# Attention on one core: the causal mask of the diagonal maxima, by mask products on TensorE or inside VectorE's fused sum-and-maximum

## The chip, the cores and the metric

The kernel runs on 1 core of one Trainium2 chip. The metric is the device time of one execution in microseconds (us), and the number to predict is the median of several executions.

## What is computed

One transformer layer in fp32: a layer norm, causal attention with 16 heads of 16 dimensions, a residual, a second layer norm, a ternary two-layer MLP with a low-rank addition, and a second residual. Input is x of (4, 2048, 256). The change concerns the attention alone:

```python
qkv = x @ W_attn + b_attn
q, k, v = jnp.split(qkv, 3, axis=2)          # 16 heads of 16
scores = jnp.einsum('bhqd,bhkd->bhqk', qh, kh) * 0.25
causal = jnp.tril(jnp.ones((S, S), dtype=bool))
scores = jnp.where(causal, scores, -jnp.inf)
probs = jax.nn.softmax(scores, axis=-1)
out = jnp.einsum('bhqk,bhkd->bhqd', probs, vh)
```

## The kernel before

Four parts run one after another: the preparation of the weights (`build_prep`), the layer norm with the q, k, v products (`build_qkv`), the attention (`build_attention`), and the output projection with the MLP (`build_mlp`). Every engine's program is written out by hand, in order, with semaphores between them.

The attention works in 16 units of one batch and four heads (`UNITS`; a pair index p = 0, 1 and a row half r = 0, 1 name the head). Queries and keys lie in chunks of 512 (`CH`), four to a unit, each of four tiles of 128. The softmax needs each query's largest score first, so every unit goes through two passes over the scores.

The maxima. A unit has 68 items (`MAXES`, `NM`). One item is formed on TensorE (`form_max`, line 1019) into one of two slots of `ps_m` (`SLOTS` = 2, two banks of 512 columns each, one per r), and VectorE takes the maximum over the keys out of it (`reduce_max`, line 967) into one column of `maxes`. 48 items lie below the diagonal: one query tile against 512 keys, for the two heads of a pair, reduced by a single VectorE instruction over 2 x 512 elements (line 976). 20 items, five to a chunk, touch the diagonal: two of width 512 (query tile 3), two that hold a piece of 384 and a piece of 128 columns (query tiles 2 and 0), and one that holds two pieces of 256 (query tile 1, both pairs). Their last 128 columns are the triangle. For these TensorE adds the mask itself: behind the scores of a piece come four bf16 products of an identity half with a mask half (line 1037), which accumulate -1e30 above the diagonal. VectorE then reduces them like the others: line 976 where the pieces are equally wide, line 979 otherwise, twice an item. `slot_filled` tells VectorE that an item is formed, and `slot_freed` tells TensorE that it is reduced. `find_max` (line 983) makes the negative maximum of a chunk; GpSimd and TensorE turn it into rows that are stored beside the queries.

The second pass. A unit has 36 steps (`STEPS`, `NS`). A full step forms the scores of one key tile for 512 queries and four heads in four banks (`scores`, line 1056, a ring `ps_s` of three banks), ScalarE takes the exponential of each bank (line 953), and TensorE multiplies the probabilities of three steps before by the values (`values`, line 1072, into `ps_acc`). Four of the 36 steps are half steps with two banks. GpSimd zeroes the triangle of the probabilities (line 891).

What sets the order. `order(s, last)` interleaves the two passes: a full step is bank 0, bank 1, one item, bank 2, values, bank 3, one more item; a half step is two banks, values, one item. The items run 40 ahead of the steps (`LEAD`), so 40 items of the first unit are formed and reduced before its first step: the opening.

The mask. `build_prep` makes `ident` and `mask` on GpSimd (lines 229 to 234) and bf16 copies of both. In `build_qkv` ScalarE's queue issues eight DMAs (line 658) that bring halves of them to the partitions where the mask products want them; they stand between the copies of the first chunk and the square root of the second (`norm.take_root(act, 1)`, line 661).

Of the kernel before, what the change touches and what calls it, by code (L numbers as in the profile page):

```python
# [25 lines left out]
BF16 = mybir.dt.bfloat16  # L26
ALU = mybir.AluOpType
# [52 lines left out]
def banks_of(s):  # L80

    return GH // STEPS[s][1]

# [95 lines left out]
def build_prep(nc, io, keep):  # L181

    with ExitStack() as ctx:
# [14 lines left out]
        w1 = t.sb("w1_sum", [P, KD, HID])  # L198
        w_qkv, w_o = t.sb("w_qkv_in", [P, KD, 3 * DIM]), t.sb("w_o_in", [P, KD, DIM])
        scale_rows = t.sb("scale_rows", [P, KD, P])  # L200
        mask = t.sb("mask", [P, P])
        ps = t.ps("ps_prep", [P, 8, 512])
        loaded, fc_in, proj_in = t.sem("prep_loaded"), t.sem("fc_in"), t.sem("proj_in")
        masked = t.sem("prep_masked")
# [21 lines left out]
        @block.gpsimd  # L226
        def _(pool):

            pool.memset(keep["ident"][:], 0.0)
            pool.memset(mask[:], 0.0).then_inc(masked, 1)  # L230
            pool.wait_ge(masked, 1)
            pool.affine_select(out=keep["ident"][:], in_=keep["ident"][:], compare_op=ALU.not_equal, fill=1.0,
                               base=0, pattern=[[-1, P]], channel_multiplier=1)
            pool.affine_select(out=mask[:], in_=mask[:], compare_op=ALU.is_ge, fill=NEG,
                               base=0, pattern=[[-1, P]], channel_multiplier=1).then_inc(masked, 1)
            pool.wait_ge(masked, 2)
            pool.tensor_copy(keep["ident_h"][:], keep["ident"][:])
            pool.tensor_copy(keep["mask_h"][:], mask[:]).then_inc(masked, 1)

        @block.vector  # L240
        def _(dve):
# [80 lines left out]
        @block.tensor  # L322
        def _(pe):
            pe.wait_ge(loaded, 16 * 9)
            pe.wait_ge(masked, 3)
            for n in range(KH):
                pe.transpose(ps[0:RANK, n // 4, (n % 4) * P:(n % 4 + 1) * P], u_in[:, n, :], keep["ident"][:])
            pe.transpose(ps[0:RANK, 2, 0:RANK], fast[:], keep["ident"][0:RANK, 0:RANK]).then_inc(done_pe, 1)

            pe.wait_ge(done_act, 1)  # L330
            pe.matmul(ps[0:RANK, 3, 0:DIM], fast_t[:], v_in[:], start=True, stop=True).then_inc(done_pe, 1)

            pe.wait_ge(done_act, 2)
            for k in range(KD):
                for half in range(2):
                    last = pe.matmul(ps[:, 4 + 2 * k + half, :], g_mat[:, k * P:(k + 1) * P],
                                     u_t[:, half * 512:half * 512 + 512], start=True, stop=True)
            last.then_inc(done_pe, 1)

            pe.wait_ge(done_act, 4)  # L340
            pe.wait_ge(chain, N_TERNARY)
            for k in range(KD):
                for half in range(2):
                    for n in range(4):
                        last = pe.transpose(ps[:, 4 + 2 * k + half, n * P:(n + 1) * P],
                                            fc_a[:, 4 * half + n, k * P:(k + 1) * P], keep["ident"][:])
                    last.then_inc(done_pe, 1)
            for n in range(KH):
                for k in range(KD):
                    col = n * DIM + k * P  # L350
                    last = pe.transpose(ps[:, col // 512, col % 512:col % 512 + P],
                                        proj_a[:, k, n * P:(n + 1) * P], keep["ident"][:])
            last.then_inc(done_pe, 1)

            pe.wait_ge(chain, N_SUM)
            for k in range(KD):
                last = pe.transpose(ps[:, 4, k * P:(k + 1) * P], scale_rows[:, k], keep["ident"][:])
            last.then_inc(done_pe, 1)
# [135 lines left out]
class Shared:  # L494
# [3 lines left out]
    def __init__(self, nc, ctx):  # L498
        t = Tensors(nc, ctx)

        self.qs, self.ks = t.sb("qs0", [P, NCH, PAIRS, CH], F32R), t.sb("ks0", [P, NCH, PAIRS, CH], F32R)
        self.vs = t.sb("vs0", [P, KT, GH, VW])
        self.v_in = t.sb("v_dense", [P, KT, GH * HD])
        self.probs = t.sb("probs", [P, RING, GH, CH])
        self.ones = t.sb("ones", [ROW, ROW])
        self.ident_half = t.sb("ident_half", [P, 2, P], BF16)
        self.mask_half = t.sb("mask_half", [P, 2, P], BF16)
        self.ones_set, self.fixed_in = t.sem("ones_set"), t.sem("fixed_in")
        self.stack_in = [[t.sem(f"stack_in{i}_{c}") for c in range(NCH)] for i in range(2)]
        self.v_loaded, self.v_ready = t.sem("v_loaded"), t.sem("v_spread")  # L510
        self.parts_stored = [t.sem(f"parts_stored{i}") for i in range(2)]
        self.v_stored = [t.sem(f"v_stored{i}") for i in range(2)]
# [31 lines left out]
            act.dma_start(ks[row:row + 1].bitcast(F32).rearrange("o c p (x e) -> o (c p x) e", e=ROW), sh.ones[:]).then_inc(sh.fixed_in, 16)  # L544

FIXED = 2 * MROWS + 2 * 2 * 2

PRELOAD, PRELOADED = 8, 4

# [1 line left out]
def build_qkv(nc, io, keep, scr, sh):  # L552

    with ExitStack() as ctx:
# [95 lines left out]
        @block.scalar  # L650
        def _(act):
            norm.take_root(act, 0)
            copy_high(act, xn_t[0], ps_t, xt_ready, xt_copied, 0)

            for r in range(2):
                for half in range(2):
                    for dst, src in ((sh.ident_half, keep["ident_h"]), (sh.mask_half, keep["mask_h"])):
                        act.dma_start(dst[ROW * r:ROW * (r + 1), half], src[ROW * half:ROW * (half + 1), :]).then_inc(sh.fixed_in, 16)
            act.wait_ge(sh.ones_set, 1)
            load_ones(act, sh, sh.ks)  # L660
            norm.take_root(act, 1)

            def body(n, used, u, left):
                if left >= 2:

                    act.wait_ge(xn_ready, n + 1)
                    load(act, n + 2, u)
                if left >= 1:

                    copy_high(act, xn_t[1 - u], ps_t, xt_ready, xt_copied, KD * (n + 1))
                if left >= 2:
                    norm.take_root(act, n + 2)
                for m in range(4):
                    act.wait_ge(qk_ready, 4 * n + m + 1)
                    if m == 0 and not zero(used):

                        act.wait_ge(parts_stored[u], 16 * 4 * used)
                    act.activation(parts[u][:, m, 0], ps_qk[:, m], ACT.Identity, bias=keep["b_qk"][:, m:m + 1]
                                   ).then_inc(qk_copied, 1)  # L680

            over_chunks(act, body)
# [44 lines left out]
def build_attention(nc, io, keep, scr, sh):  # L727

    with ExitStack() as ctx:
# [1 line left out]
        qs = [sh.qs, t.sb("qs1", [P, NCH, PAIRS, CH], F32R)]  # L731
        ks = [sh.ks, t.sb("ks1", [P, NCH, PAIRS, CH], F32R)]
        vs = [sh.vs, t.sb("vs1", [P, KT, GH, VW])]
        probs, ident_half, mask_half, stack_in = sh.probs, sh.ident_half, sh.mask_half, sh.stack_in
        maxes = [t.sb(f"maxes{i}", [P, 2, PAIRS, TT, NCH]) for i in range(2)]
        neg_max = [t.sb(f"neg_max{i}", [P, 2, PAIRS * TT]) for i in range(2)]
        max_parts = [t.sb(f"max_parts{i}", [P, 2, MROWS, PAIRS * TT], F32R) for i in range(2)]
# [229 lines left out]
        def _(dve):  # L967
            def reduce_max(n, k):
                c, pieces = MAXES[k]
                slot = k % SLOTS  # L970
                dve.wait_ge(slot_filled, NM * n + k + 1)
                if pieces[0][4] == pieces[-1][4]:
                    (_, tt, i, _, width) = pieces[0]
                    pairs = slice(pieces[0][0], pieces[-1][0] + 1)
                    banks = ps_m[:, 2 * slot:2 * slot + 2].rearrange("q r (p x) -> q r p x", x=width)
                    last = dve.tensor_reduce(maxes[c % 2][:, :, pairs, tt, i], banks, AX.X, ALU.max)  # L976
                else:
                    for p, tt, i, col, width in pieces:
                        last = dve.tensor_reduce(maxes[c % 2][:, :, p, tt, i], ps_m[:, 2 * slot:2 * slot + 2, col:col + width],  # L979
                                                 AX.X, ALU.max)  # L980
                last.then_inc(slot_freed, 1)

            def find_max(n, c):
# [34 lines left out]
        def _(pe):  # L1018
            def form_max(n, par, k):
# [8 lines left out]
                for p, tt, i, col, width in pieces:  # L1028
                    for r in range(2):
                        rows = slice(ROW * r, ROW * r + TERMS)  # L1030
                        last = pe.matmul(ps_m[:, 2 * slot + r, col:col + width], qs[par][rows, c, p, tt * P:(tt + 1) * P],  # L1031
                                         ks[par][rows, i, p, 0:width], start=True, stop=(i < c), skip_group_check=True)
                    if i == c:
                        for half in range(2):
                            for r in range(2):
                                rows = slice(ROW * r, ROW * (r + 1))
                                last = pe.matmul(ps_m[:, 2 * slot + r, col + width - P:col + width], ident_half[rows, half],  # L1037
                                                 mask_half[rows, half], start=False, stop=(half == 1), skip_group_check=True)
                last.then_inc(slot_filled, 1)

            def turn_rows(n, c, k):
# [345 lines left out]
def build_layer(nc, io):  # L1387
    with ExitStack() as ctx:
# [8 lines left out]
            "b_v": t.sb("b_v", [P, DIM]),  # L1397
            "b_o": t.sb("b_o", [P, DIM]),
            "ident": t.sb("ident", [P, P]),
            "ident_h": t.sb("ident_h", [P, P], BF16),  # L1400
            "mask_h": t.sb("mask_h", [P, P], BF16),
        }
        scr = {
            "q": nc.dram_tensor("q_scr", [BATCH, PARTS, DIM, SEQ], F32).ap(),
# [38 lines left out]
```

## Time and profile before

| | us |
|---|---|
| median of 3 executions | 2171.63 |
| lowest and highest | 2161.71, 2176.84 |
| the profiled execution | 2175.73 |
| its span, first to last instruction | 2174.0 |
| TensorE busy | 2060.0 (95%) |
| VectorE busy | 1818.3 (84%) |
| ScalarE busy | 1460.1 (67%) |
| GpSimd busy | 473.6 (22%) |

### The profile page before, as it was taken

The numbers are of one execution on the slowest core, as the hardware profiler recorded it, in microseconds if no ns is written. First come the engines' busy times: TensorE is split into PE (matmuls) and PEld (weight loads), VectorE is DVE, ScalarE is ACT, GpSimd is POOL, SyncE is SP. The second block draws the span as 40 slices with busy tenths as digits, with TensorE's granted clock in tenths as the row PEclk, the third lists the DMA queues.
The fourth block names the chain that finished last, engine by engine and source line by source line (L and its number), as shares of the span: only waits on it lengthen the run. The fifth ranks groups of instructions, "written<-read, shape, count | busy, mean of one in ns | idle before, by whom it ended". The sixth has DMA issues, their size and how long they took to land. (4 is left out here: it accounts for less than half of the span.)

```text
span 2174.0 us, 40441 instructions
## 1 busy us (share of the span) xinstructions
PE 2060.0 (95%) x15605; PEld 1202.4 (55%) x15605; DVE 1818.3 (84%) x2365; ACT 1460.1 (67%) x2800; POOL 473.6 (22%) x637
## 2 busy tenths in 40 slices
PE   3999799999999999999999999999999949999998
PEld 2887354544545445454444544444454228888887
DVE  6898888888888888888888888888888018998996
ACT  1333078887878788787787887878878625555554
POOL 0000011110111101111011111111111027776674
PEclk8999589999999999999999999999999759999999
DMA  2799121311213212122221212212120023232320
GB/s 86 260 315 342 63 58 37 78 46 51 56 37 79 52 51 56 37 73 51 59 55 37 67 49 66 50 42 63 46 69 17 11 82 85 81 101 84 88 78 30
DMA packets 162977, 167.92 MB, mean 77 GB/s; under 512 B 74704, under 2 KB 102880, under 8 KB 162784
## 3 DMA queue, kind: packets, MB, share of 16 engines
q1 hardware_dynamic: 154112, 157.72, 24.9%
q10 hardware_dynamic: 8672, 7.60, 1.2%
q8 instruction: 123, 2.02, 0.4%
q14 instruction: 70, 0.57, 0.1%
HBM read 95.77 MB, written 67.63 MB: 75 GB/s over the span
## 5 line engine op out<-in xcount | busy, mean ns | idle before, releaser
L953 ACT ACTIVATE probs<-ps_s 128x512 f32<-128x512 f32 x2176 | 1144.5, 601 | 291.7 <-PE ps_s L1068 282.3
L976 DVE TENSOR_REDUCE maxes<-ps_m 128x2 f32<-128x1024 f32 (+1 forms) x960 | 1136.5, 1218 | 139.6 <-PE ps_m L1031 104.0
L1068 PE MATMUL ps_s<-qs,ks 50*128 50x512 f32 (+3 forms) x2560 | 810.3, 416 | 8.6 <-ACT probs L953 8.5
L1031 PE MATMUL ps_m<-ks,qs 48*128 48x512 f32 (+3 forms) x2560 | 715.9, 426 | 15.6 <-DVE maxes L976 9.6
L1068 PEld LDWEIGHTS ps_s<-qs,ks 50*128 50x128 f32 x2560 | 404.0, 189 | 510.4 <-ACT probs L953 461.5
L1087 PE MATMUL ps_acc<-probs,vs 128*32 128x512 f32 (+3 forms) x5120 | 598.5, 549 | 0.7
L1031 PEld LDWEIGHTS ps_m<-ks,qs 48*128 48x128 f32 x2560 | 362.4, 190 | 105.8 <-issue 49.5
L891 POOL TENSOR_SCALAR_AFFINE_SELECT probs<-probs 128x512 f32<-128x512 f32 x256 | 157.6, 637 | 753.0 <-ACT probs L953 753.0
L1037 PE MATMUL ps_m<-mask_half,ident_half 64*128 64x128 bf16 x2048 | 207.4, 227 | 0.0
L1087 PEld LDWEIGHTS ps_acc<-probs,vs 128*32 128x32 f32 x5120 | 109.3, 109 | 160.1 <-issue 98.1
L1240 POOL TENSOR_TENSOR hid<-square,hid 128x512 fp32r<-128x512 f32 x128 | 174.6, 1372 | 105.8 <-DVE square L1251 93.4
L979 DVE TENSOR_REDUCE maxes<-ps_m 128x2 f32<-128x768 f32 (+1 forms) x256 | 161.6, 685 | 28.7 <-PE ps_m L1037 28.2
L1360 PE MATMUL ps_y<-w,hid 128*128 128x256 f32 x1024 | 131.8, 284 | 6.7 <-POOL hid L1240 6.7
L879 POOL CAST max_parts<-neg_max 128x16 fp32r<-128x16 f32 x64 | 12.7, 198 | 573.9 <-DVE neg_max L985 573.9
L1313 ACT ACTIVATE relu<-ps_h 128x512 f32<-128x512 f32 x128 | 76.4, 597 | 88.8 <-PE ps_h L162 80.0
L1360 PEld LDWEIGHTS ps_y<-w,hid 128*128 128x128 f32 x1024 | 125.4, 188 | 11.5 <-POOL hid L1240 10.1
L1251 DVE TENSOR_TENSOR square<-relu 128x512 f32<-128x512 f32 x96 | 96.5, 1012 | 26.4 <-ACT relu L1313 25.4
L160 PE MATMUL ps_h<-mxn_t,w 128*128 128x512 f32 x256 | 102.3, 400 | 1.5 <-DVE mxn_t L491 1.4
L1037 PEld LDWEIGHTS ps_m<-mask_half,ident_half 64*128 64x128 bf16 x2048 | 94.2, 98 | 15.7 <-issue 5.2
L162 PE MATMUL ps_h<-mxn_t,w 128*128 128x512 f32 x256 | 101.8, 398 | 0.0
L161 PE MATMUL ps_h<-mxn_t,w 128*128 128x512 f32 x256 | 101.6, 397 | 0.0
L1318 ACT ACTIVATE hid<-relu 128x512 fp32r<-128x512 f32 x128 | 81.0, 633 | 4.1
(129 smaller groups left out, 1635.7 us busy)
## 6 DMA issues: line engine op xcount, KB each, us to landing
qs<-q_scr SPq DMA_DIRECT2D x384, 64.0 KB, 2.7
ks<-k_scr SPq DMA_DIRECT2D x384, 64.0 KB, 2.7
q_scr<-probs SPq DMA_DIRECT2D x32, 512.0 KB, 4.4
k_scr<-probs SPq DMA_DIRECT2D x32, 512.0 KB, 5.6
o_scr<-acc_sb SPq DMA_DIRECT2D x64, 256.0 KB, 2.9
v_scr<-probs SPq DMA_DIRECT2D x16, 512.0 KB, 6.1
v_dense<-v_scr SPq DMA_DIRECT2D x16, 512.0 KB, 4.6
o_in<-o_scr SPq DMA_DIRECT2D x32, 256.0 KB
```

Of the source, the lines that this page charges most:

```text
L160: pe.matmul(out, sh, mh, start=start, stop=False)
L162: return pe.matmul(out, sl, mh, start=False, stop=stop)
L891: pool.affine_select(out=tile, in_=tile, compare_op=ALU.is_ge, fill=0.0, base=0, pattern=[[0, GH], [1, P]], channel_multiplier=-1).then_in ...
L953: act.activation(probs[:, s % RING, x], ps_s[:, k % BANKS], ACT.Exp).then_inc(ring_taken, 1)
L976: last = dve.tensor_reduce(maxes[c % 2][:, :, pairs, tt, i], banks, AX.X, ALU.max)
L979: last = dve.tensor_reduce(maxes[c % 2][:, :, p, tt, i], ps_m[:, 2 * slot:2 * slot + 2, col:col + width], AX.X, ALU.max)
L1031: last = pe.matmul(ps_m[:, 2 * slot + r, col:col + width], qs[par][rows, c, p, tt * P:(tt + 1) * P], ks[par][rows, i, p, 0:width], start=T ...
L1037: last = pe.matmul(ps_m[:, 2 * slot + r, col + width - P:col + width], ident_half[rows, half], mask_half[rows, half], start=False, stop=(h ...
L1068: last = pe.matmul(ps_s[:, k % BANKS, at:at + width], ks[u][rows, j // TT, p, j % TT * P:(j % TT + 1) * P], qs[u][rows, c, p, q0:q0 + widt ...
L1087: last = pe.matmul(ps_acc[h * VW:(h + 1) * VW, q0:q0 + width], vs[u][:, j, h], probs[:, s % RING, h % banks_of(s), at:at + width], start=( ...
L1240: pool.tensor_tensor(hid[:, 1, m], square[:, m], hid[:, 0, m].bitcast(F32), ALU.subtract).then_inc(low_done, 1)
L1360: last = pe.matmul(ps_y[:, i, (tt % 2) * DIM:(tt % 2 + 1) * DIM], hid[:, a, m, tt * P:(tt + 1) * P], keep["w2"][:, m], start=(m == 0 and a ...
```

## The change

VectorE adds the mask to the diagonal pieces while it takes their maximum: `tensor_tensor_reduce` computes (scores + mask) x 1.0, writes it to a scratch tile `sums_masked`, and puts the maximum over it into one column of `maxes`. It takes one head at a time, so each piece needs two of them (r = 0, 1). The mask is a tile of 128 x 512, zero but for the triangle in its last 128 columns, and a piece of width w reads its last w columns. Since scratch is used again by the next diagonal item, VectorE waits before each such item until its own last instruction of the item before is done (`slot_freed`). TensorE's mask products go, and with them the halves of identity and mask, their bf16 copies and their eight DMAs.

```diff
@@ build_prep, GpSimd
-            pool.memset(mask[:], 0.0).then_inc(masked, 1)
+            pool.memset(keep["mask"][:], 0.0).then_inc(masked, 1)
...
-            pool.affine_select(out=mask[:], in_=mask[:], compare_op=ALU.is_ge, fill=NEG,
+            pool.affine_select(out=keep["mask"][:, CH - P:], in_=keep["mask"][:, CH - P:], compare_op=ALU.is_ge, fill=NEG,
                                base=0, pattern=[[-1, P]], channel_multiplier=1).then_inc(masked, 1)
-            pool.wait_ge(masked, 2)
-            pool.tensor_copy(keep["ident_h"][:], keep["ident"][:])
-            pool.tensor_copy(keep["mask_h"][:], mask[:]).then_inc(masked, 1)
@@ build_qkv, ScalarE
-            for r in range(2):
-                for half in range(2):
-                    for dst, src in ((sh.ident_half, keep["ident_h"]), (sh.mask_half, keep["mask_h"])):
-                        act.dma_start(dst[ROW * r:ROW * (r + 1), half], src[ROW * half:ROW * (half + 1), :]).then_inc(sh.fixed_in, 16)
             act.wait_ge(sh.ones_set, 1)
             load_ones(act, sh, sh.ks)
@@ build_attention
+        sums_masked = t.sb("sums_masked", [P, 4, CH])
@@ build_attention, VectorE, reduce_max
                 dve.wait_ge(slot_filled, NM * n + k + 1)
-                if pieces[0][4] == pieces[-1][4]:
-                    (_, tt, i, _, width) = pieces[0]
-                    pairs = slice(pieces[0][0], pieces[-1][0] + 1)
-                    banks = ps_m[:, 2 * slot:2 * slot + 2].rearrange("q r (p x) -> q r p x", x=width)
-                    last = dve.tensor_reduce(maxes[c % 2][:, :, pairs, tt, i], banks, AX.X, ALU.max)
+                if pieces[0][2] < c:
+                    (p, tt, i, _, _), = pieces
+                    last = dve.tensor_reduce(maxes[c % 2][:, :, p, tt, i], ps_m[:, 2 * slot:2 * slot + 2], AX.X, ALU.max)
                 else:
+
+                    if NM * n + k > 0:
+                        dve.wait_ge(slot_freed, NM * n + k)
                     for p, tt, i, col, width in pieces:
-                        last = dve.tensor_reduce(maxes[c % 2][:, :, p, tt, i], ps_m[:, 2 * slot:2 * slot + 2, col:col + width],
-                                                 AX.X, ALU.max)
+                        for r in range(2):
+                            last = dve.tensor_tensor_reduce(sums_masked[:, 2 * pieces.index((p, tt, i, col, width)) + r, 0:width], ps_m[:, 2 * slot + r, col:col + width],
+                                                            keep["mask"][:, CH - width:], 1.0, NEG, ALU.add, ALU.max,
+                                                            maxes[c % 2][:, r, p, tt, i:i + 1])
                 last.then_inc(slot_freed, 1)
@@ build_attention, TensorE, form_max
-                                         ks[par][rows, i, p, 0:width], start=True, stop=(i < c), skip_group_check=True)
-                    if i == c:
-                        for half in range(2):
-                            for r in range(2):
-                                rows = slice(ROW * r, ROW * (r + 1))
-                                last = pe.matmul(ps_m[:, 2 * slot + r, col + width - P:col + width], ident_half[rows, half],
-                                                 mask_half[rows, half], start=False, stop=(half == 1), skip_group_check=True)
+                                         ks[par][rows, i, p, 0:width], start=True, stop=True, skip_group_check=True)
```

How instructions stand on VectorE at the first diagonal of the opening (items of width 512 and 512, then the two of 384 and 128 columns). Before:

```order
350 L976 TENSOR_REDUCE maxes<-ps_m 128x2 [waits slot_filled] x2
351 L979 TENSOR_REDUCE maxes<-ps_m 128x2 [waits slot_filled]
352 L979 TENSOR_REDUCE maxes<-ps_m 128x2
353 L979 TENSOR_REDUCE maxes<-ps_m 128x2 [waits slot_filled]
354 L979 TENSOR_REDUCE maxes<-ps_m 128x2
```

Here a diagonal item is one or two reductions, each over both heads. In the changed kernel, from the second item of width 512 to the end of the first of 384 and 128 columns, the same engine has (ISA is the name these rows give to the parts of a `tensor_tensor_reduce`):

```order
354 L974 ISA sums_masked,maxes<-ps_m,mask 128x512 [waits slot_freed,slot_filled]
355 L974 ISA maxes 128x1
356 L974 ISA sums_masked,maxes<-ps_m,mask 128x512
357 L974 ISA maxes 128x1
358 L974 ISA sums_masked,maxes<-ps_m,mask 128x384 [waits slot_freed,slot_filled]
359 L974 ISA maxes 128x1
360 L974 ISA sums_masked,maxes<-ps_m,mask 128x384
361 L974 ISA maxes 128x1
362 L974 ISA sums_masked,maxes<-ps_m,mask 128x128
363 L974 ISA maxes 128x1
364 L974 ISA sums_masked,maxes<-ps_m,mask 128x128
365 L974 ISA maxes 128x1
```

An item of width 512 has become four instructions, one of 384 and 128 columns eight: each sum-and-maximum is followed by one that writes a single column of `maxes`.

TensorE before, the first chunk of the opening (items of width 512, 512, 384 and 128):

```order
816 L1031 MATMUL ps_m<-ks,qs 128x512 [waits stack_in0_0,fixed_in]
817 L1031 MATMUL ps_m<-ks,qs 128x512
818 L1037 MATMUL ps_m<-mask_half,ident_half 128x128 x4
819 L1031 MATMUL ps_m<-ks,qs 128x512 x2
820 L1037 MATMUL ps_m<-mask_half,ident_half 128x128 x4
821 L1031 MATMUL ps_m<-ks,qs 128x384 [waits slot_freed]
822 L1031 MATMUL ps_m<-ks,qs 128x384
823 L1037 MATMUL ps_m<-mask_half,ident_half 128x128 x4
824 L1031 MATMUL ps_m<-ks,qs 128x128 x2
825 L1037 MATMUL ps_m<-mask_half,ident_half 128x128 x4
```

And the same place of the changed kernel:

```order
816 L1027 MATMUL ps_m<-ks,qs 128x512 [waits stack_in0_0,fixed_in]
817 L1027 MATMUL ps_m<-ks,qs 128x512 x3
818 L1027 MATMUL ps_m<-ks,qs 128x384 [waits slot_freed]
819 L1027 MATMUL ps_m<-ks,qs 128x384
820 L1027 MATMUL ps_m<-ks,qs 128x128 x2
```

The mask products are gone and nothing else moved; the waits for a free slot stand where they stood.

## Rows read from the trace of the kernel before

**Rows 1.** Busy time by stretch: opening and body of the attention's maxima.

```profile
core 0: us, PE busy (x) PEld busy (x) DVE busy (x) ACT busy (x) POOL busy (x), PEclk, DMA share, GB/s
223.00:275.00 52.00, 40.93 (x211) 20.90 (x212) 48.51 (x51) 4.32 (x9) 3.09 (x8) 0.50 0.07 24
275.00:1688.00 1413.00, 1408.88 (x11849) 686.34 (x11851) 1252.14 (x1290) 1134.82 (x2216) 191.58 (x383) 1.00 0.20 53
```

**Rows 2.** VectorE groups by form: busy us, mean ns, idle before them.

```profile
L976 DVE TENSOR_REDUCE maxes<-ps_m 128x2 f32<-128x1024 f32 x896 | 1059.9, 1218 | 125.3 <-PE ps_m L1031 104.0 <-PE ps_m L1037 16.2
L979 DVE TENSOR_REDUCE maxes<-ps_m 128x2 f32<-128x768 f32 x128 | 122.1, 954 | 28.7 <-PE ps_m L1037 28.2
L976 DVE TENSOR_REDUCE maxes<-ps_m 128x4 f32<-128x1024 f32 x64 | 78.2, 1221 | 14.3 <-PE ps_m L1037 14.3
L979 DVE TENSOR_REDUCE maxes<-ps_m 128x2 f32<-128x256 f32 x128 | 53.2, 416 | 0.0
...
L644 DVE TENSOR_TENSOR probs<-ps_v,b_v 128x256 f32<-128x256 f32 x64 | 22.7, 414 | 1.3 <-PE ps_v L162 1.3
...
L491 DVE TENSOR_TENSOR xn_t<-ps_t,xn_t 128x512 fp32r<-128x512 f32 x32 | 20.7, 681 | 4.1 <-ACT xn_t L484 4.0
```

**Rows 3.** Mask products on TensorE, by form.

```profile
L1037 PE MATMUL ps_m<-mask_half,ident_half 64*128 64x128 bf16 x2048 | 207.4, 227 | 0.0
```

**Rows 4.** TensorE timeline, value products alone: the start of each step.

```profile
1034.63 1.07 PE L1087 MATMUL ps_acc<-probs,vs 128*32 128x384 f32 x16
1037.24 0.64 PE L1087 MATMUL ps_acc<-probs,vs 128*32 128x256 f32 x8
1039.76 1.06 PE L1087 MATMUL ps_acc<-probs,vs 128*32 128x512 f32 x8
1042.62 1.06 PE L1087 MATMUL ps_acc<-probs,vs 128*32 128x512 f32 x8
...
1053.85 1.07 PE L1087 MATMUL ps_acc<-probs,vs 128*32 128x512 f32 x8
```

**Rows 5.** VectorE timeline: steps below the diagonal, then the diagonal of a chunk.

```profile
1024.51 2.36 DVE L976 TENSOR_REDUCE maxes<-ps_m 128x2 f32<-128x1024 f32 x2 [0.31 <-PE ps_m L1031]
1027.12 2.36 DVE L976 TENSOR_REDUCE maxes<-ps_m 128x2 f32<-128x1024 f32 x2 [0.24 <-PE ps_m L1031]
...
1041.84 2.48 DVE L979 TENSOR_REDUCE maxes<-ps_m 128x2 f32<-128x768 f32 x4 [0.72 <-PE ps_m L1037]
1044.71 2.36 DVE L976 TENSOR_REDUCE maxes<-ps_m 128x4 f32<-128x1024 f32 x2 [0.38 <-PE ps_m L1037]
...
1055.63 1.23 DVE L976 TENSOR_REDUCE maxes<-ps_m 128x2 f32<-128x1024 f32 x1 [0.41 <-PE ps_m L1031]
```

**Rows 6.** VectorE timeline of the opening, second chunk.

```profile
231.65 0.17 DVE L985 TENSOR_REDUCE neg_max<-maxes 128x16 f32<-128x16 f32 x1
231.74 10.36 DVE L976 TENSOR_REDUCE maxes<-ps_m 128x2 f32<-128x1024 f32 x9
242.44 2.48 DVE L979 TENSOR_REDUCE maxes<-ps_m 128x2 f32<-128x768 f32 x4 [0.35 <-PE ps_m L1037]
```

**Rows 7.** VectorE timeline in the q, k, v part: two-operand and small instructions.

```profile
63.75 0.16 DVE L406 TENSOR_TENSOR tmp_attn<-rstd_attn 128x4 f32<-128x4 f32 x1
63.94 0.16 DVE L408 TENSOR_TENSOR tmp_attn<-tmp_attn,var_attn 128x4 f32<-128x4 f32 x1
...
68.48 1.41 DVE L644 TENSOR_TENSOR probs<-ps_v,b_v 128x256 f32<-128x256 f32 x4
70.03 1.29 DVE L491 TENSOR_TENSOR xn_t<-ps_t,xn_t 128x512 fp32r<-128x512 f32 x2
```

**Rows 8.** Timeline of ScalarE, its queue and VectorE around the eight DMAs.

```profile
47.52 0.54 ACTq L658 DMA_DIRECT2D ident_half<-ident_h  x1
...
50.70 0.17 DVE L401 TENSOR_SCALAR var_attn<-mv_attn 128x4 f32<-128x4 f32 x1
...
51.97 0.62 ACTq L658 DMA_DIRECT2D mask_half<-mask_h  x1
52.63 2.55 ACTq L544 DMA_DIRECT2D ks<-ones  x4
55.22 0.20 ACT L421 ACTIVATE root_attn<-var_attn 128x4 f32<-128x4 f32 x1 [7.12 <-issue]
```

More of the change, by code:

```diff
@@ L200, in build_prep @@
         scale_rows = t.sb("scale_rows", [P, KD, P])
-        mask = t.sb("mask", [P, P])
         ps = t.ps("ps_prep", [P, 8, 512])
@@ L324, in _ @@
             pe.wait_ge(loaded, 16 * 9)
-            pe.wait_ge(masked, 3)
+            pe.wait_ge(masked, 2)
             for n in range(KH):
@@ L505, in __init__ @@
         self.ones = t.sb("ones", [ROW, ROW])
-        self.ident_half = t.sb("ident_half", [P, 2, P], BF16)
-        self.mask_half = t.sb("mask_half", [P, 2, P], BF16)
         self.ones_set, self.fixed_in = t.sem("ones_set"), t.sem("fixed_in")
@@ L544, in load_ones @@
             act.dma_start(ks[row:row + 1].bitcast(F32).rearrange("o c p (x e) -> o (c p x) e", e=ROW), sh.ones[:]).then_inc(sh.fixed_in, 16)
-FIXED = 2 * MROWS + 2 * 2 * 2
+FIXED = 2 * MROWS
 PRELOAD, PRELOADED = 8, 4
@@ L733, in build_attention @@
         vs = [sh.vs, t.sb("vs1", [P, KT, GH, VW])]
-        probs, ident_half, mask_half, stack_in = sh.probs, sh.ident_half, sh.mask_half, sh.stack_in
+        probs, stack_in = sh.probs, sh.stack_in
+        sums_masked = t.sb("sums_masked", [P, 4, CH])
         maxes = [t.sb(f"maxes{i}", [P, 2, PAIRS, TT, NCH]) for i in range(2)]
@@ L1399, in build_layer @@
             "ident": t.sb("ident", [P, P]),
-            "ident_h": t.sb("ident_h", [P, P], BF16),
-            "mask_h": t.sb("mask_h", [P, P], BF16),
+            "mask": t.sb("mask", [P, CH]),
         }
```

## The prediction

> **What bounds the kernel now.** I read the busy times by stretch first. The opening of the attention (52 us) is VectorE's: it is busy 48.5 us of it, and TensorE's clock is 0.50, its lower level of 1.2 GHz, while it waits for slots. The body (1413 us) looks like TensorE's, busy 1409 us, at clock 1.00 [rows 1]. But VectorE is busy 1252 us of the same 1413, so it has only 161 us to spare, 11%. In such a case the mean share decides nothing, and I look at the steps.
>
> A step's length is the distance between starts of value products: 2.61 us from 1034.63 to 1037.24 for a step below the diagonal, 2.86 us from 1039.76 to 1042.62 for one that holds two items of 384 and 128 columns, and 14.09 us for the five steps from 1039.76 to 1053.85 [rows 4]. On VectorE a step below the diagonal is two reductions and a gap of 0.24 us that ends when TensorE has formed the next item; at the diagonal the gap is 0.38 to 0.72 us and ends with a mask product of line 1037 [rows 5]. So below the diagonal VectorE waits for TensorE by a quarter of a microsecond per step, and at the diagonal by a little more: the mask products do sit on the path, but VectorE is almost as late. Over the trace VectorE's idle time that line 1037 ends is 16.2 + 28.2 + 14.3 = 58.7 us [rows 2]. TensorE's 207.4 us of mask products [rows 3] are no measure of what they cost, since two row halves run side by side and most of it lies beside other products.
>
> **What the masks cost on the path.** Five steps with diagonal items took 14.09 us against 5 x 2.61 = 13.05: 1.04 us, or 0.21 a step [rows 4]. They hold seven diagonal items, so one chunk (five items) costs about 0.7 us, and 64 chunks 45 us. That is the most that taking them away can bring, if nothing becomes later.
>
> **What VectorE pays instead.** All distances are from start to start where no wait stands between, which is what a queue pays. Before, one reduction of 1024 elements: nine take 10.36 us [rows 6], the last counting in full with 1.22 us [rows 2], so (10.36 - 1.22) / 8 = 1.14 us. An item of 384 and 128 columns is two reductions: with 0.08 us of overlap each, (0.954 - 0.08) + (0.416 - 0.08) = 1.21 us [rows 2]. A chunk's five diagonal items: 3 x 1.14 + 2 x 1.21 = 5.84 us.
>
> After, each piece is done once per head. The nearest rows for one such instruction are additions or subtractions of a bank in PSUM and a tile in SBUF: 512 columns, two in 1.29 us of which the last is 0.68, so 0.61 us; 256 columns, four in 1.41 us, the last 0.41, so 0.33 us [rows 2, 7]. The slope is 1.09 ns a column; 384 columns then cost 0.47 us and 128 cost 0.19 us. A chunk has four of each width: 4 x (0.61 + 0.47 + 0.33 + 0.19) = 6.40 us. That is already more than before, since 16 instructions replace 7.
>
> Second, the order shows a further instruction behind each of the 16, which puts one column into `maxes`. No row shows one like it. From below: a reduction of 16 values, after which the next instruction starts 0.09 us later (231.65 to 231.74) [rows 6]; from above: the read waits until the sum has run out (0.07 us, the overlap that is lost between 0.68 and 0.61) and the next waits for the read's full 0.16 us, which is a small instruction's duration [rows 7], together 0.23 us. The lowest bound is that it costs nothing. I take 0.125 us, halfway between 0.09 and 0.16 (the read waits for the sum but nothing waits for the read), because no row decides between these two: 16 x 0.125 = 2.0 us.
>
> Third, the new wait on `slot_freed`: VectorE waits for the end of its own last instruction. With such waits, small instructions start 0.19 us apart (63.75 to 63.94) [rows 7], against 0.09 without one [rows 6]: 0.10 to 0.12 us, five times a chunk, 0.55 us. Behind the waiting instruction in VectorE's queue stand the other items, `neg_max` (for which GpSimd and then TensorE's row transposition wait, many steps ahead of need) and the reciprocals.
>
> The Trainium skill speaks against charging that wait: by its page "VectorE: DVE Perf Modes", section "The DRAIN you can't avoid", an instruction drains the pipe before the next in any case, and a semaphore between two adds nothing. The trace does not agree for small instructions (0.19 us with a wait, 0.09 without) [rows 6, 7]; by the page's rule the sum below would be 64 x 0.55 = 35 us less. The same page, in "Rules for kernel authors", advises fewer instructions over fused ones, which is what the count of 32 for 7 here goes against.
>
> Sum: 6.40 + 2.0 + 0.55 = 8.95 us a chunk against 5.84, so 3.11 us more, and 64 x 3.11 = 199 us more work on VectorE.
>
> **What hides part of it.** There are only two slots, so an item that is late holds up TensorE two items later; TensorE stands in front of the slot and with it the next bank, ScalarE's exponentials and the value products, and steps below the diagonal can't catch up, because they are bound by the loop of TensorE and ScalarE (their 2.61 us has 0.24 us of gap on VectorE, 9%). So only idle time right at the diagonal items is filled. That is the 58.7 us ended by line 1037, less some 5 us before the very first item, so 54 us, and one gap behind the last diagonal item of each chunk, 0.41 us at 1055.63 [rows 5], 64 x 0.41 = 26 us. Together 80 us. 199 - 80 = 119 us longer. The mask products' own gain is inside this: it is the idle time that VectorE now fills.
>
> The three diagonals of the opening are in the sum as others are; there VectorE is last by the whole.
>
> **The rest.** ScalarE's queue issues the eight DMAs from 47.52 until 52.6, then those of the ones; the square root for the second chunk, whose variance was ready at 50.87, starts at 55.22 after no wait but "issue" [rows 8]. Without the eight it starts at about 51.0: 4 us earlier, and VectorE's second normalisation with it. I take 4 us off; it may be 0 if the later stores of this part set its end. GpSimd's mask is four times as wide, but two conversions are gone, at the start of the kernel where nothing waits for it: nothing. The MLP is as before.
>
> Against the profiled execution: 2175.7 + 119 - 4 = 2290.7 us. The median of the runs is 4 us lower than that execution, by which the sum is 2286.6; the difference is well inside the 15 us between the lowest and the highest run, and I put 2290.
>
> **Rivals.**
>
> *Serial reads.* Each sum-and-maximum and each read run to their ends: 0.23 us instead of 0.125, 16 x 0.105 x 64 = 108 us more: 2400. For it: a value that is read out must be complete. Against: VectorE's other neighbours overlap by 0.07 to 0.09 us without a wait.
>
> *Half the rate.* If the fused instruction takes two cycles a column where it has a second tensor and a running maximum, 4 x 1280 columns x 1.09 ns = 5.6 us a chunk more, 357 us: about 2650. No row shows such an instruction; the additions of [rows 7] run at one column per 1.09 ns with an SBUF tensor beside PSUM. The Trainium skill has such a rule on its page "Vector Engine (DVE) Microarchitecture Reference", section "Points that are easy to get wrong", for two sources in SBUF wider than bf16 with an accumulator; here one source is PSUM, and no run so far shows which way it falls.
>
> *Faster, VectorE hidden.* If the one-column instruction and the wait cost nothing, VectorE's excess is 6.40 - 5.84 = 0.56 us a chunk, less than the 80 / 64 = 1.25 us of idle time that stands at the diagonals. Then TensorE is last there, and what counts is the mask products' 0.7 us: 2175.7 - 45 - 4 = 2127. The point from which it decides is (1.25 - 0.56) / 16 = 0.04 us per read, wait included. Against it: every small instruction in the trace costs at least 0.09.
>
> *Little change.* The read costs the 0.09 us and the wait nothing, and more idle time is filled than I count, say 1.9 of the 2.5 us that the body's 161 us are per chunk: 6.40 + 1.44 - 5.84 - 1.9 = 0.1 us a chunk: about 2180.
>
> *The clock falls.* While VectorE needs 3.9 us for a step of two 384-and-128 items, TensorE works under 2 us of it. In the opening, waiting for slots, its clock is at 1.2 GHz [rows 1]. If it fell at each diagonal, a step's value products of 1.06 us would take twice as long, three steps a chunk, 64 x 3 x 1.06 = 204 us at most: up to 2495.
>
> **Chances.** Forecast, with its own range of 2235 to 2350: 0.56. Serial reads: 0.18. Half the rate: 0.06. Clock: 0.05. Cheaper than forecast but over 1% slower (reads at 0.09 us or less and more hidden, 2195 to 2235): 0.07. Little change: 0.04. Faster: 0.04. The range 2210 to 2420 leaves out the last two, half the rate and most of the clock's case. About 1% is what a measurement of this kernel can tell from no change: faster 0.04, same 0.04, slower 0.92.
>
> **What would show it.** Right: line 974 with 1024 long instructions of 0.68, 0.54, 0.41 and 0.28 us and 1024 short ones; VectorE busy above 95% in the body; no idle time ended by a mask product; TensorE's weight loads waiting for `maxes` of line 974; steps at diagonals of 3.0 to 3.9 us, below them 2.6 as before; the square root near 51 us. Wrong: long instructions of twice these lengths, a clock below 1.00 in the body, or steps of 2.6 us at the diagonal.

## The result, and the profile after

| | us |
|---|---|
| median after (4 executions, 2197.2 to 2214.9) | 2206.53 |
| median before, beside it | 2174.24 |
| ratio | 1.0142, 95% interval 1.0107 to 1.0177 |
| the same pair measured again later (6 executions) | 2207.72, ratio 1.0174, 1.0130 to 1.0218 |
| profiled execution, its span | 2214.9, 2213.1 |

The change makes the kernel 1.4% slower, 32 us, where 2290 us was forecast, 116 us slower, with a range that began at 2210. The sign was right and the size was not. Beside the kernel before as it ran then, the second comparison gives 40 us. Ratios are formed from fast executions alone (one of e3_before_no_masks, 2159.11 us, and one of the kernel before beside g1 to g3, 2194.71 us, were slow), so they are not exactly the quotients of the medians.

The second stretch of [rows 1], in the profile after:

```profile
275.00:1688.00 1413.00, 1357.37 (x9563) 594.71 (x9565) 1272.58 (x2727) 1102.14 (x2149) 183.95 (x371) 0.99 0.20 53
```

TensorE is busy 51 us less of this stretch and VectorE only 20 us more: 1273 of 1413, 90%, not the 95% that I named. (The changed kernel runs longer, so the same window holds a little less of its work.) VectorE's groups at the diagonal, by form:

```profile
L974 DVE CUSTOM_DVE_ANT_0 sums_masked<-ps_m,mask 128x512 f32<-128x512 f32 x256 | 166.7, 689 | 23.5 <-PE ps_m L1027 7.9 <-DVE maxes L974 1.0 <-issue 0.7
...
L974 DVE DVE_READ_ACCUMULATOR2_ANT maxes<- 128x1 f32 x1024 | 84.9, 83 | 0.0
...
L974 DVE CUSTOM_DVE_ANT_0 sums_masked<-ps_m,mask 128x128 f32<-128x128 f32 x256 | 63.5, 285 | 0.0
```

The long instructions last what the additions of [rows 2] do, one column per 1.05 ns (0.689 and 0.285 us for 512 and 128 columns), so the rival of half the rate is out. The reads have 83 ns each, 85 us in all, but the sum of busy times hides where they lie. The timeline of the opening shows it (start, duration):

```profile
226.93 0.56 DVE L974 CUSTOM_DVE_ANT_0 sums_masked<-ps_m,mask 128x384 f32<-128x384 f32 x1
227.41 0.08 DVE L974 DVE_READ_ACCUMULATOR2_ANT maxes<- 128x1 f32 x1
227.41 0.55 DVE L974 CUSTOM_DVE_ANT_0 sums_masked<-ps_m,mask 128x384 f32<-128x384 f32 x1
...
228.31 0.08 DVE L974 DVE_READ_ACCUMULATOR2_ANT maxes<- 128x1 f32 x1
228.54 0.56 DVE L974 CUSTOM_DVE_ANT_0 sums_masked<-ps_m,mask 128x384 f32<-128x384 f32 x1
```

A read starts at the same time as the next long instruction (both 227.41), so its 83 ns are no price. Whether it moves that start at all can't be told here; e5_no_read measures it. Where there is a wait, from 228.31 to 228.54, 0.23 us pass that would not without it. Such an item takes 1.61 us (226.93 to 228.54), of which the wait is a seventh.

The starts of steps at a diagonal, to be read beside [rows 4], are 2.98 and 3.16 us apart here:

```profile
1067.19 1.06 PE L1077 MATMUL ps_acc<-probs,vs 128*32 128x512 f32 x8
1070.17 1.06 PE L1077 MATMUL ps_acc<-probs,vs 128*32 128x512 f32 x8
1073.33 1.06 PE L1077 MATMUL ps_acc<-probs,vs 128*32 128x512 f32 x8
```

and TensorE's loads now stand behind a slot that line 974 has not freed:

```profile
PEld ps_m L1027 <- DVE maxes L974: 127.3, 180, 1.7
```

The cleanest ruler is the distance between the last `neg_max` of one unit and of the next, since a unit is the same work each time. After (two units):

```profile
981.54 0.21 DVE L981 TENSOR_REDUCE neg_max<-maxes 128x16 f32<-128x64 f32 x1
1075.60 0.21 DVE L981 TENSOR_REDUCE neg_max<-maxes 128x16 f32<-128x64 f32 x1
```

Before:

```profile
955.20 0.21 DVE L985 TENSOR_REDUCE neg_max<-maxes 128x16 f32<-128x64 f32 x1
1046.98 0.21 DVE L985 TENSOR_REDUCE neg_max<-maxes 128x16 f32<-128x64 f32 x1
```

94.06 against 91.78 us: 2.28 us a unit, 34 us over the 15 distances between the first such instruction and the last. The first comes 8 us later (320.51 against 312.46). The eight DMAs that are gone give nothing back in this pair of profiles: the first product of the maxima starts at 223.19 us, and at 222.84 before.

### The profile page after: what moved, and what is told of

Same layout as the page of the kernel before. It is cut to its first block and busy times, and to the rows that moved or that the text cites. A ratio compares the mean times of both kernels' runs of the same rounds, so it can differ in the third digit from the quotient of the medians.

```text
span 2213.1 us, 38254 instructions
## 1 busy us (share of the span) xinstructions
PE 2038.7 (92%) x13557; PEld 1123.0 (51%) x13557; DVE 1880.7 (85%) x3965; ACT 1461.4 (66%) x2800; POOL 471.9 (21%) x635
## 5 line engine op out<-in xcount | busy, mean ns | idle before, releaser
L967 DVE TENSOR_REDUCE maxes<-ps_m 128x2 f32<-128x1024 f32 x768 | 911.0, 1218 | 99.7 <-PE ps_m L1027 92.4
L1058 PE MATMUL ps_s<-qs,ks 50*128 50x512 f32 (+3 forms) x2560 | 778.6, 406 | 9.5 <-ACT probs L946 9.5
L1027 PE MATMUL ps_m<-ks,qs 48*128 48x512 f32 (+3 forms) x2560 | 667.2, 426 | 75.6 <-DVE maxes L974 61.1
L974 DVE CUSTOM_DVE_ANT_0 sums_masked<-ps_m,mask 128x512 f32<-128x512 f32 (+3 forms) x1024 | 446.8, 488 | 51.1 <-PE ps_m L1027 7.9
L1027 PEld LDWEIGHTS ps_m<-ks,qs 48*128 48x128 f32 x2560 | 311.2, 191 | 213.2 <-DVE maxes L974 127.3
L974 DVE DVE_READ_ACCUMULATOR2_ANT maxes<- 128x1 f32 x1024 | 84.9, 83 | 0.0
L989 DVE RECIPROCAL recip<-sums 128x16 f32<-128x16 f32 x64 | 15.5, 243 | 65.4 <-DMA sums<-acc_sb 65.4
```

The lines of the kernel that those rows point to most:

```text
L974: last = dve.tensor_tensor_reduce(sums_masked[:, 2 * pieces.index((p, tt, i, col, width)) + r, 0:width], ps_m[:, 2 * slot + r, col:col + w ...
L1058: last = pe.matmul(ps_s[:, k % BANKS, at:at + width], ks[u][rows, j // TT, p, j % TT * P:(j % TT + 1) * P], qs[u][rows, c, p, q0:q0 + widt ...
```

## The experiments

Each ran beside the kernel before on one chip: e1 to e4 on one, e5 to e8 on another, g1 to g3 on a third. "Unit" is the distance just shown, read in each profile. It is the surest comparison across chips, since the medians also carry TensorE's mean granted clock, which differs from execution to execution. In the ten executions of the changed kernel it runs from 0.970 (2196.87 us) to 0.960 (2210.75 to 2214.90 us), about 1.7 us for each 0.001; 37 executions of the kernel before lie on a line of 1.6 us for each 0.001. Differences "at equal clock" below are my estimates by these two lines. They assume that a change acts beside the clock and not through it.

| run | what it is | median us | ratio to before | unit us |
|---|---|---|---|---|
| changed kernel | | 2206.53 | 1.0142 | 94.06 |
| e1_two_scratch | changed, the wait made idle | 2135.35 | 0.9807 | 90.38 |
| e2_before_wait | before, wait added | 2184.45 | 1.0036 | 92.25 |
| e3_before_no_masks | before, no mask products | 2136.59 | 0.9791 | 89.71 |
| e4_both_masks | changed, mask products kept | 2215.06 | 1.0172 | 94.17 |
| e5_no_read | changed, no read of the maximum | 2204.48 | 1.0124 | 93.12 |
| e6_dmas_back | changed, eight DMAs kept | 2218.57 | 1.0188 | 93.87 |
| e7_no_masks_wait | e3 with the wait | 2160.26 | 0.9918 | 90.42 |
| e8_last_unit_busy | e1 with products for nobody in the last unit | 2141.14 | 0.9828 | 90.43 |

**The wait alone, taken off the changed kernel** (e1_two_scratch). Two halves of scratch, used in turn; the wait is for the item before the last one, which is done by then.

```diff
-        sums_masked = t.sb("sums_masked", [P, 4, CH])
+        sums_masked = t.sb("sums_masked", [P, 8, CH])
...
-                    if NM * n + k > 0:
-                        dve.wait_ge(slot_freed, NM * n + k)
+                    half = 4 * (sum(j % NM in DIAGONAL_ITEMS for j in range(NM * n + k)) % 2)
+                    if NM * n + k > 1:
+                        dve.wait_ge(slot_freed, NM * n + k - 1)
```

> The changed kernel with twice the scratch, used in turn by the diagonal items, so that VectorE waits for the end of the item before the last one and not of the last one. Theory V (VectorE's time at the diagonals sets the loss: per chunk four of each width, 6.6 us, plus five waits of 0.22 us, 1.1 us): the waits are free, VectorE's time falls by 320 x 0.22 = 70 us, its excess over the kernel before is 0.8 us a chunk and is filled by idle time, and the time falls below both kernels, to 2136 to 2165 us. Theory N (the loss comes from the sixteen fused instructions themselves, and the wait lies in time that is lost anyway): 2195 to 2210 us, as the changed kernel.

Measured 2135.35 us, 71 us under the changed kernel and 1.9% under the kernel before. The unit is 3.68 us shorter, 59 us over 16, and 59 us is also the difference at equal clock; the rest of the 71 is a higher clock (0.966 to 0.972, against 0.960 to 0.968). The wait was the whole loss and more: without it the change is a gain. In its timeline the four 384 and 128 pieces follow at their plain distances; the next item starts 0.21 us after the last and not 0.21 + 0.23:

```profile
224.69 0.28 DVE L976 CUSTOM_DVE_ANT_0 sums_masked<-ps_m,mask 128x128 f32<-128x128 f32 x1
224.90 0.08 DVE L976 DVE_READ_ACCUMULATOR2_ANT maxes<- 128x1 f32 x1
224.90 0.55 DVE L976 CUSTOM_DVE_ANT_0 sums_masked<-ps_m,mask 128x384 f32<-128x384 f32 x1
```

**The same wait, added to the kernel before** (e2_before_wait).

```diff
                 dve.wait_ge(slot_filled, NM * n + k + 1)
+                if pieces[0][2] == c and NM * n + k > 0:
+                    dve.wait_ge(slot_freed, NM * n + k)
```

> The kernel before with nothing but the added wait of VectorE for its own last item, ahead of each diagonal item. Theory V: 320 waits of 0.22 us are 70 us of VectorE, of which the idle time at the diagonals (about 80 us) hides most: 2174 to 2190 us. Theory N: a wait for the engine's own last instruction costs nothing: 2174 us. If the waits lie on the path in full: 2244 us.

2184.45 us, 5 us over before (ratio 1.0036, 1.0011 to 1.0061), and 7 us by the unit and at equal clock. The same waits that cost 59 us there cost 7 here: most of each falls into the idle time that ends with a mask product.

**TensorE's mask products alone** (e3_before_no_masks). The four products behind each diagonal piece are left out and the reductions kept, so the maxima of diagonal pieces run over later keys as well.

> The kernel before without the mask products on TensorE (line 1037); the reductions stay, so the maxima of the diagonal pieces run over later keys too, and the mask is left out of them. What the mask products cost on the path by themselves. By the step lengths of the trace of before (0.21 us a step, 0.7 us a chunk): 45 us, 2120 to 2140 us. If VectorE's reductions are last there and the products lie beside them: 2165 to 2174 us.

2136.59 us, 43 us less. That looks like the estimate of 45 from step lengths, but the unit is only 2.07 us shorter, 33 us over 16, and the difference at equal clock is 35 us: the estimate was about 10 us too high. VectorE, unmasked, is hidden here: this is about the floor that taking the masks away can reach. e1's median is at it, but only because its executions had a higher clock: its unit is 0.67 us longer, and at equal clock it is 28 us under before where e3 is 35.

**Both at once** (e4_both_masks): the fused VectorE code with the mask products kept.

> The changed VectorE code with the mask products of TensorE kept (and their eight DMAs): the mask is added twice. Theory V: VectorE is last at the diagonals of the changed kernel, so TensorE has room for the products and only a part of their 45 us shows: 2215 to 2235 us. If the two costs simply add: 2250 us.

2215.06 us, 9 us over the changed kernel, and its unit is only 0.11 us longer (2 us over 16; this kernel also has the eight DMAs). Where VectorE is last, TensorE's products are nearly free. Removing them gained nothing as long as the wait stood.

**The read of the maximum** (e5_no_read).

```diff
-                                                            maxes[c % 2][:, r, p, tt, i:i + 1])
+                                                            None)
```

> The changed kernel without the instruction that reads the running maximum out (the diagonal pieces' maxima are left out; the tile of maxima is set to zero once instead). By the prediction's term (0.125 us for each of 1024): 128 us less VectorE time, and a time near 2120 us. Theory V, by the starts in the trace of the changed kernel (a read lies inside the overlap of two long instructions): VectorE's starts are 0.61, 0.48, 0.34 and 0.21 us apart as before, and the time is that of the changed kernel, 2198 to 2212 us.

2204.48 us beside 2206.53: the medians show no difference. But they hide one: e5 ran at a lower clock (0.950 to 0.961). At 0.961 one execution took 2195.38 us, where the changed kernel took 2210.75 to 2214.90 us at 0.960; over all four the difference at equal clock is 17 us, and the unit is 0.94 us shorter, 15 us over 16. The starts confirm it. An item of 384 and 128 columns takes 1.56 us from its first instruction to the next item's, where it took 1.61 us with four reads:

```profile
225.82 0.56 DVE L975 CUSTOM_DVE_ANT_0 sums_masked<-ps_m,mask 128x384 f32<-128x384 f32 x1
227.38 0.42 DVE L975 CUSTOM_DVE_ANT_0 sums_masked<-ps_m,mask 128x256 f32<-128x256 f32 x1
```

So neither forecast holds in full. A read costs about 0.015 us, 15 us in all and not 128, and most of its 83 ns lies inside the overlap.

**A step rule.** Units with the fused instructions fit one rule: a step lasts the longer of 2.61 us and the two items that VectorE has in it. With the wait, items take 1.46, 1.61 and 1.60 us (widths 512, 384 and 128, 256): 0.31 + 0.61 + 0.13 over the floor, 1.05 us a chunk, 67 us. (Two items of width 512 make 2.92 us, two of 384 and 128 make 3.22, and the one of 256 makes 2.74 with an item of 1.14 below the diagonal.) The changed kernel lies 70 us over e3, by the medians and by the units (4.35 us each). For e1, whose items of 384 and 128 take 1.38 us without the wait, the rule gives 0.15 us a chunk over the floor, 0.6 us a unit, and 0.67 us are measured. I then let the rule predict a new mix (e7_no_masks_wait), e3 with the edit of e2.

> The kernel before without mask products (the mask is left out of the maxima), and with the added wait of VectorE before each diagonal item. Step rule (a step lasts the longer of 2.61 us and its two items on VectorE): items of 1.36 us pair to 2.72, items of 1.43 to 2.86, so 0.36 us a chunk, 23 us over the kernel without masks: 2155 to 2168 us. If the waits lie on the path in full, 70 us: 2207 us. If they are hidden: 2137 us.

2160.26 us, 24 over e3, against 23 by the rule. This agreement is luck. The unit grows by 0.71 us, 11 us over 16, where the rule had said 4 x 0.36 = 1.44 us, and at equal clock the whole is 13 us longer. Of the 27 us between the two profiled executions, 5 lie ahead of the attention's first product and 8 behind the last maxima, where the code is the same. The rule had been fed with a wait of 0.22 us, but behind a `tensor_reduce` it is shorter:

```profile
995.33 2.56 DVE L978 TENSOR_REDUCE maxes<-ps_m 128x2 f32<-128x1024 f32 x2 [0.25 <-PE ps_m L1033]
997.99 2.68 DVE L981 TENSOR_REDUCE maxes<-ps_m 128x2 f32<-128x768 f32 x4
1000.77 1.23 DVE L978 TENSOR_REDUCE maxes<-ps_m 128x4 f32<-128x1024 f32 x1
```

The pairs take 2.66 us (995.33 to 997.99) and 2.78 us (to 1000.77), not 2.72 and 2.86, so a wait is about 0.19 us. With these lengths the rule gives 0.22 us a chunk, 0.88 us a unit, still more than the 0.71 measured. It orders the kernels rightly and is good to a few tenths of a microsecond a unit.

**The eight DMAs** (e6_dmas_back, and again as g2_dmas_back beside g1_after_again, five rounds each on one chip).

> The changed kernel with the eight DMAs of the identity and mask halves put back on ScalarE's queue (nothing reads what they bring). The prediction's term: the second square root starts near 55 us and not near 51, and the whole is 4 us longer, 2211 us. Rival (what is won at the start is waited for later in the q, k, v part): the square root is late, the first diagonal item starts at about 224 us all the same, and the time is that of the changed kernel, 2198 to 2212 us.

> The changed kernel with the eight DMAs put back, on the same chip as the changed kernel. If the DMAs cost what the square root's delay says: 4 us over it, up to 6. If they cost nothing: within 2 us of it. If the 12 to 14 us between the earlier runs were theirs: 12 us over it.

2218.57 us, and in the second comparison 2219.77 us against 2207.72 us: 12 us more with the DMAs, twice, where I had expected 4. The delay at the start is as I read it: the second square root starts at 55.15 us in g2 and at 50.54 us in g1, and at the first product of the maxima 5 us are left, 226.41 against 221.24 us. But that product moves by as much between executions of the same code up to there (222.84, 223.62, 222.90 and 227.86 us in before, e2, e3 and e7, all with the eight DMAs). The two profiled executions can't place the rest, since they are 35 us apart and not 12 (2231.48, the slowest of g2, and 2196.87, the fastest of g1). TensorE's clock tells more: the executions with the DMAs have 0.948 to 0.965, those without 0.960 to 0.970. At equal clock the DMAs cost 1 us in e6 and 3 us in g2. The rest of the 12 us goes with the lower clock, and whether the DMAs cause that clock stays open.

> The changed kernel as it is, beside the next two on one chip, so that a few microseconds can be told apart: 2200 to 2212 us.

> The two scratch halves again, on the same chip: the step rule and the distance of its units (90.4 us against 94.05) say 59 us under the changed kernel, the first runs say 71: 2135 to 2150 us.

Two scratch halves again on that chip: 2143.48 us, ratio 0.9892 (0.9842 to 0.9942), 64 us under the changed kernel, 58 at equal clock. It is the fastest version here that masks as the reference does.

**A dead end** (e8_last_unit_busy). In the last unit there are no maxima left to form, and in the profile of before a step of the second pass then takes 4.07 us and not 2.61, as ScalarE's rows show:

```profile
1716.27 2.08 ACT L953 ACTIVATE probs<-ps_s 128x512 f32<-128x512 f32 x4 [1.99 <-PE ps_s L1068]
1720.33 2.08 ACT L953 ACTIVATE probs<-ps_s 128x512 f32<-128x512 f32 x4 [1.99 <-PE ps_s L1068]
```

TensorE's clock is 0.50 there, after 0.99 in the 20 us before:

```profile
1710.00:1730.00 20.00, 18.70 (x64) 4.89 (x60) 0.25 (x1) 10.79 (x22) 0.00 (x0) 0.50 0.05 15
```

I let TensorE form products that nobody reads in place of the missing items.

> The kernel with two scratch halves, and in the last unit, where no maxima are left to form, TensorE forms products that nobody reads in their place. Theory C (in the last unit TensorE's granted clock falls from 1.00 to 0.50, and a step of the second pass then takes 4.07 us and not 2.61): the clock stays at 1.00, the part behind the last maxima is 467 us long or a little shorter, and the time falls by 5 to 20 us, to 2115 to 2130 us, with less spread. Rival: the products only add to TensorE's work: 2135 to 2145 us.

2141.14 us, not faster than e1; the rival forecast this. In the profile of e1 the clock happened to stay at 1.00 through the attention's end, and with the added products it still fell once: it was 0.66 on average from 1660 to 1680 us, with TensorE busy 18.5 of the 20 us. So these products did not hold the clock in that profile. What lets it fall there stays open.

## Why the prediction was wrong

The prediction's sum was 199 us more for VectorE, less 80 us hidden, less 4 us at the start. Term by term:

1. *The one-column instruction, 16 x 0.125 = 2.0 us a chunk, 128 us.* This is the step that failed. Measured: about 0.015 us each, 0.23 us a chunk, 15 us, by e5's unit and starts. I bounded it by instructions that follow each other, and took the middle of two values (0.09 and 0.16) that both stood above the truth; the truth lies near the lowest bound, nothing. I had given that case few chances although the point from which the faster rival decides (0.04 us a read, wait included) was only 0.085 us away from my value.
2. *The wait, 0.55 us a chunk.* Right in kind and half its size: 0.22 us each and not 0.11, 1.1 us a chunk, 70 us in all. I had taken it from small instructions, where the wait exposes less. A long one with a tail of 0.07 to 0.08 us of overlap loses that and about 0.15 more.
3. *The long instructions, 6.40 us a chunk.* Measured from start to start, with the reads inside: 4 x (0.615 + 0.48 + 0.345 + 0.21) = 6.60 us; without them (e5) 4 x (0.608 + 0.470 + 0.331 + 0.198) = 6.43 us. Right.
4. *The sum* is then 6.60 + 1.10 - 5.84 = 1.86 us a chunk, 119 us and not 199.
5. *What is hidden, 80 us.* The 15 units between the first `neg_max` and the last grew by 34 us and the time to the first by 8, so 119 - 42 = 77 us were hidden. Right, though this is a difference of sums: no row shows the hidden time by itself.
6. *The start, 4 us.* The square root is where I put it. At equal clock the DMAs were worth 1 to 3 us.

These terms can't be added up as a proof, since the hidden part was itself read from the measured units. The 42 us, less about 4 at the start, are 38, where the two comparisons measured 32 and 40 us. In the first pair of profiles the part behind the last maxima, with the same code, is 8 us shorter after (477 against 485 us), at a higher clock there, and the units that a fall of the clock made longer add about 5.

The two wrong terms worked against each other, and the right sign is partly luck. With the true price of a read and my wait the sum would have been 6.40 + 0.23 + 0.55 - 5.84 = 1.34 us a chunk, 86 us, of which my 80 were hidden and 4 won at the start: 2 us, no change. By this estimate, what makes the kernel slower is the half of the wait that I had left out, 35 us.

The rivals. Serial reads and half the rate are refuted by the profile. *Faster, VectorE hidden* named the right mechanism and the right condition, and its premise on the read nearly held; it failed on the wait. With the wait gone (e1) the condition holds: 44 and 25 us under the kernel before by the medians, 28 and 26 at equal clock, where it had forecast 49, because the mask products were worth 35 us and not 45. *Little change* priced the read at 0.09 us and the wait at nothing, both wrong. What came, cheaper than forecast but over 1% slower (2195 to 2235), I had given 0.07, and for another reason (reads at 0.09 us or less, more hidden). *The clock falls* happened a little: two of fifteen units after are over 2 us longer than 94.06 (from 1169.54 to 1266.20 it is 96.66 us, at a mean clock of 0.96), and none before.

The Trainium skill's rule that a semaphore between two VectorE instructions adds nothing ("VectorE: DVE Perf Modes", section "The DRAIN you can't avoid") does not hold here: 0.23 us in the timeline, and 59 us between the changed kernel and e1 by the units. What a rule of that page foresees, that an instruction with an accumulator output is two (section "Two Vector instructions with no wait between them"), is what the trace shows; it says nothing on the price of the second, which is about 0.015 us here.

## What to carry to other kernels

An instruction's duration in a profile is not its price: take the distance between starts in a stretch without waits, and where no row shows an instruction, keep zero as a live end of the range and say from which price the sign turns. A median can hide a difference when the clock differs too: put the granted clock beside each execution, and compare units inside a profile. The wait before a scratch tile is written again is dear where its engine is last, even if nobody reads the tile (no run here leaves it out altogether); a second copy of the tile turned this change from 1.4% slower into 1 to 2% faster. Where one engine waits for another step by step, compare sums per step with the step's floor, not totals over the kernel: the same waits cost 7 us or 59 us, by what stood beside them.

## What the runs showed of the hardware

- The read of VectorE's accumulator, 83 ns in the profile, lies for the most part inside the overlap of two long instructions: taking 1024 of them away saved about 0.015 us each (e5: an item of four reads 1.56 us and not 1.61, the unit 93.12 us and not 94.06).
- A VectorE wait for its own last instruction, with a semaphore that this instruction raises, puts 0.23 us between starts that would follow at once, behind the fused sum-and-maximum; behind a `tensor_reduce` about 0.19 us (e7).
- TensorE's clock fell from 1.00 to 0.50 (1.2 GHz) in the last unit of the attention, when the products of the maxima were gone (before: TensorE busy 17.9 of the 20 us ahead of the fall and 18.7 of the 20 us after it). The stretch behind the last maxima grows as the clock of its first 60 us falls: 467 us at a mean of 0.97 (e1), 469 at 0.94 (g1), 477 at 0.77 (changed kernel), 485 at 0.68 (before), 496 at 0.53 (e4). This is a large part of the differences between executions of one kernel (changed kernel and g1: 8 of 18 us), and a reason to compare units inside a profile before medians.
